# Causal attention in a decoder kernel: rotary projection with even and odd features in two halves of one bank

## The reference, cut to what matters

```python
def _rope(x, freqs):
    xr, xi = x[..., ::2], x[..., 1::2]          # even and odd features of a head
    yr = xr * cos(freqs) - xi * sin(freqs)
    yi = xr * sin(freqs) + xi * cos(freqs)
    return stack([yr, yi], axis=-1).reshape(x.shape)

KQV = einsum('bsd,ed->bse', X, W_KQV)           # X: (16, 256, 256), 16 heads of 16 features
K, Q, V = split(KQV)                            # then to (batch, head, position, feature)
Q, K = _rope(Q, freqs), _rope(K, freqs)
scores = einsum('bhqd,bhkd->bhqk', Q, K) / sqrt(16), -inf above the diagonal
heads = einsum('bhqk,bhkd->bhqd', softmax(scores), V)
return einsum('bsd,ed->bse', heads_joined, W_O)
```

## Time and profile before

| what | value |
|---|---|
| time before | 4390.62 us, median of 3 executions (4387.88 to 4397.72) |
| profiled execution, its own time | 4384.22 us |
| its span | 4382.0 us |
| granted TensorE clock, mean of the span | 0.896 |
| busy over the span | PE 3550.0 us (81%), DVE 3046.5 us (70%), ACT 1118.1 us (26%), POOL 1578.6 us (36%) |
| causal stage | from the first weight load at 33.0 us to the last write of x_all at about 576 us |

### The profile page before, as it was taken

One profiled execution on the slowest core, in us unless ns is written; L12 is line 12 of the kernel. 1 busy time (PEld: TensorE's weight loads), 2 busy tenths in 40 slices (PEclk: granted clock), 3 DMA queues, 4 the chain that ended last, 5 costly groups with the idle time before them and its releaser, 6 DMA issues. The chain is left out here.

```text
span 4382.0 us, 100620 instructions
## 1 busy us (share of the span) xinstructions
PE 3550.0 (81%) x34160; PEld 2968.7 (68%) x34161; DVE 3046.5 (70%) x11891; ACT 1118.1 (26%) x2415; POOL 1578.6 (36%) x1612
## 2 busy tenths in 40 slices
PE   3999938885688998898999896788868866799991
PEld 2777725554688888888888885455546654699991
DVE  5777735665999999999999995799973444422222
ACT  0333314442222222222222220444431110122220
POOL 1222212220666666666666674323200000111115
PEclk9999968887799999999999998899987965899995
DMA  4333333332000000000000000433310014455555
GB/s 118 93 90 94 81 73 96 90 95 85 2 2 3 2 2 2 2 2 2 2 2 2 3 2 20 108 91 93 91 29 20 7 33 125 134 181 182 180 180 158
DMA packets 246561, 282.58 MB, mean 64 GB/s; under 512 B 35225, under 2 KB 188321, under 8 KB 245825
## 3 DMA queue, kind: packets, MB, share of 16 engines
q1 hardware_dynamic: 239681, 260.04, 20.7%
q0 software_dynamic: 6528, 17.83, 1.4%
HBM read 201.31 MB, written 76.48 MB: 63 GB/s over the span
## 5 line engine op out<-in xcount | busy, mean ns | idle before, releaser
L1100 POOL TENSOR_TENSOR peer_hot_v<-peer_hot_e,peer_parts 80x512 bf16<-80x512 bf16 x768 | 1038.0, 1378 | 494.5 <-DVE peer_hot_e L1138 467.1
L946 PE MATMUL peer_ps_u<-peer_up,peer_g 128*128 128x256 f32 x2048 | 531.6, 406 | 0.6 <-DVE x_all L1255 0.6
L927 PEld LDWEIGHTS peer_ps_h<-peer_xnT,peer_down 128*128 128x128 f32 x4096 | 511.6, 197 | 17.5 <-DMA peer_down<-in_peer_down 2.8
L927 PE MATMUL peer_ps_h<-peer_xnT,peer_down 128*128 128x128 f32 x4096 | 511.0, 279 | 2.4 <-DMA peer_down<-in_peer_down 2.4
L937 PE MATMUL peer_ps_w<-peer_hot_v,peer_hot_u 80*128 80x32 bf16 x12288 | 348.0, 177 | 191.3 <-DVE peer_g L1150 96.1
L937 PEld LDWEIGHTS peer_ps_w<-peer_hot_v,peer_hot_u 80*128 80x128 bf16 x12288 | 335.2, 97 | 219.4 <-DVE peer_hot_u L1142 119.8
L946 PEld LDWEIGHTS peer_ps_u<-peer_up,peer_g 128*128 128x128 f32 x2048 | 396.9, 203 | 51.6 <-issue 1.0
L2050 POOL DMA_INDIRECT x_all<-moe_xn_rows,moe_column x72 | 68.3, 949 | 1007.8 <-DVE moe_column L2118 1002.8
L1023 ACT ACTIVATE peer_g<-peer_ps_h 128x512 f32<-128x512 f32 x256 | 152.9, 597 | 892.5 <-PE peer_ps_h L927 892.5
L1142 DVE TENSOR_TENSOR peer_hot_u<-peer_count,peer_uvT 80x2048 bf16<-80x2048 bf16 x256 | 344.8, 1347 | 0.0
L1959 PE MATMUL moe_ps_h<-x_all,moe_w 128*128 128x128 f32 x2304 | 270.1, 276 | 0.0
(11 more groups left out here) (364 smaller groups left out, 7215.5 us busy)
## 6 DMA issues: line engine op xcount, KB each, us to landing
moe_w<-in_moe_w SPq DMA_DIRECT2D x144, 512.0 KB, 4.4
causal_qs<-causal_qscratch SPq DMA_DIRECT2D x32, 384.0 KB, 3.8
cross_qs<-cross_qscratch SPq DMA_DIRECT2D x32, 384.0 KB, 3.5
band_qs<-band_qscratch SPq DMA_DIRECT2D x32, 384.0 KB, 3.8
moe_y_rows<-x_all SPq DMA_DIRECT2D x72, 128.0 KB, 1.7
moe_w<-in_moe_w SPq DMA_DIRECT2D x8, 1024.0 KB, 6.8
causal_qscratch<-causal_part SPq DMA_DIRECT2D x32, 192.0 KB, 2.0
causal_kscratch<-causal_part SPq DMA_DIRECT2D x32, 192.0 KB, 2.0
```

The source lines that it names most:

```text
L927: mm = nc.tensor.matmul(ps_h[:, n % 2, k * P:(k + 1) * P], down[:, c, 4 * n + k, :], xnT[:, par, c, :], start=(c == 0), stop=(c == DC - 1))
L946: mm = nc.tensor.matmul(ps_u[:], g[:, par, v, :], up[:, v, :], start=(v == 0), stop=(v == EV - 1))
L1100: ins = nc.gpsimd.tensor_tensor(hot_v[0:SEL, n % RING, part], hot_e[0:SEL, n % RING], w, ALU.mult)
```

## The change

Weights of q and k are laid out so that the first 128 columns are the even features of all 16 heads and the last 128 the odd ones. One job now covers all of q, and one all of k: its products with even and with odd features fill the two halves of one bank (four f32 products a job, as before, but two jobs a batch element where there were four). The projections with swapped weights and their two weight loads go. VectorE multiplies the whole bank (128x512) by a cosine and by a sine table, then forms the even half by a subtraction and the odd half by an addition, each 128x256, f32 only. The bf16 high part is no longer a second addition on VectorE: ScalarE copies it, 128x512, from `full`, and GpSimd waits for ScalarE's semaphore `high_ready`. GpSimd's three operations are 128x512 in place of 128x256. The jobs stand at steps 2 and 5 instead of 2, 4, 6 and 8. The scratch writes keep their number and size. Each `stack` issues eight DMAs of half the size where it issued four, and the two stacks of element 1 have an additional wait on `s1_done`. The order of the 96 rows of `qs` and `ks` changes alike on both sides.

```diff
-    JOBS = [(qk, c) for c in range(DC) for qk in range(2)]
+    JOBS = [(0, None), (1, None)] if rope else [(qk, c) for c in range(DC) for qk in range(2)]
+    WIDE = DC * S if rope else S
...
-    STACKED = 16 * (1 + len(KRUNS))
+    STACKED = 16 * (1 + len(KRUNS)) * (DC if rope else 1)
...
-        names = ["wq", "wqs", "wk", "wks", "wv"] if rope else ["wq", "wk", "wv"]
-        w = {n: sb(n, [P, DC, D]) for n in names}
+        w = {n: sb(n, [P, DC, D]) for n in ("wq", "wk", "wv")}
...
-        PROJECT, OUT, VALUES, STACK = (2, 4, 6, 8), 10, 12, 10
+        PROJECT, OUT, VALUES, STACK = (2, 5) if rope else (2, 4, 6, 8), 10, 12, 10
...
+                    if rope:
+                        for e in range(DC):
+                            half = slice(e * S, (e + 1) * S)
+                            if qk == 0:
+                                for slot, slots, a in QRUNS:
+                                    sp.dma_start(qscratch[par, e, slot:slot + slots].rearrange("s p t -> p s t"),
+                                                 part[:, j, a:a + 1, half].broadcast_to((P, slots, S))).then_inc(parts_out, 16)
+                            else:
+                                sp.dma_start(kscratch[par, e].rearrange("s p t -> p s t"),
+                                             part[:, j, :, half]).then_inc(parts_out, 16)
+                        return
...
+                    if rope:
+                        if isinstance(b, int) and b == 1:
+                            sp.wait_ge(s1_done, CH * c + 1)
+                        def rows(ap):
+                            return ap.rearrange("s (r h) t -> (s r) h t", h=HEADS)[:, mine, :]
+                        for e in range(DC):
+                            at = e * ROWS // DC
+                            sp.dma_start(qs[at:at + ROWS // DC, par, mine, :], rows(qscratch[par, e])).then_inc(stacked[c], 16)
+                            for slot, slots, a in KRUNS:
+                                sp.dma_start(ks[at + slot * HALFD:at + (slot + slots) * HALFD, par, mine, :],
+                                             rows(kscratch[par, e, a:a + slots])).then_inc(stacked[c], 16)
+                        return
...
-                    mine = [("wq", "wqs"), ("wk", "wks")] if rope else [("wq",), ("wk",)]
-                    for k, name in enumerate(mine[qk]):
+                    for k, part_of in enumerate(range(DC) if rope else (chunk,)):
                         for c in range(DC):
                             mm = nc.tensor.matmul(ps_p[:, (j + 1) % 2, k * S:k * S + n],
-                                                  w[name][:, c, chunk * P:(chunk + 1) * P], src[:, par, c, :],
+                                                  w[("wq", "wk")[qk]][:, c, part_of * P:(part_of + 1) * P], src[:, par, c, :],
...
                     if rope:
+                        act.wait_ge(proj_used, NJ * b + j + 1)
+                        wait(act, split_ready, NJ * b + j - 1)
+                        wait(act, parts_out, OUTS * b)
+                        nc.scalar.activation(part[:, j, 0, :], full[:, j % 2, :], ACT.Copy).then_inc(high_ready, 1)
                         return
...
-                    pool.wait_ge(proj_used, NJ * b + j + 1)
+                    pool.wait_ge(high_ready if rope else proj_used, NJ * b + j + 1)
...
-                    nc.vector.tensor_tensor(rot[:, j % 2, 0, :], bank[:, 0:S], tab[cs][:], ALU.mult)
-                    steps.link(nc.vector.tensor_tensor(rot[:, j % 2, 1, :], bank[:, S:2 * S], tab[sn][:], ALU.mult))
+                    by_cos, by_sin = rot[:, j % 2, 0], rot[:, j % 2, 1]
+                    nc.vector.tensor_tensor(by_cos, bank, tab[cs][:].unsqueeze(1).broadcast_to((P, DC, S)), ALU.mult)
+                    steps.link(nc.vector.tensor_tensor(by_sin, bank, tab[sn][:].unsqueeze(1).broadcast_to((P, DC, S)), ALU.mult))
 
                     wait(dve, split_ready, NJ * b + j - 1)
-                    wait(dve, parts_out, OUTS * b)
-                    for dst in (full[:, j % 2, :], part[:, j, 0, :]):
-                        ins = nc.vector.tensor_tensor(dst, rot[:, j % 2, 0, :], rot[:, j % 2, 1, :], ALU.add)
-                    ins.then_inc(proj_used, 1)
+                    nc.vector.tensor_tensor(full[:, j % 2, 0:S], by_cos[:, 0, :], by_sin[:, 1, :], ALU.subtract)
+                    nc.vector.tensor_tensor(full[:, j % 2, S:2 * S], by_sin[:, 0, :], by_cos[:, 1, :],
+                                            ALU.add).then_inc(proj_used, 1)
...
+def _even_odd(np, wt):
+    v = wt.reshape(wt.shape[0], HEADS, HD // 2, 2)
+    return np.transpose(v, (0, 3, 2, 1)).reshape(wt.shape)
```

More of the change, by code:

```diff
@@ L155, in attention_stage @@
     CH = HEADS // DC
-    JOBS = [(qk, c) for c in range(DC) for qk in range(2)]
+    JOBS = [(0, None), (1, None)] if rope else [(qk, c) for c in range(DC) for qk in range(2)]
     NJ = len(JOBS)
+    WIDE = DC * S if rope else S
+    HALFD = HD // 2
     QRUNS = [(0, 3, 0), (3, 2, 1), (5, 1, 2)]
@@ L188, in attention_stage @@
             maskf = sb("maskf", [P, 2, P])
-            rot = sb("rot", [P, 2, 2, S])
+            rot = sb("rot", [P, 2, 2, DC, S])
             nload += 5
@@ L207, in attention_stage @@
         xnT = sb("xnT", [P, 2, DC, S])
-        full = sb("full", [P, 2, S])
-        rest = sb("rest", [P, S])
-        part = sb("part", [P, NJ, 3, S], BF16)
+        full = sb("full", [P, 2, WIDE])
+        rest = sb("rest", [P, WIDE])
+        part = sb("part", [P, NJ, 3, WIDE], BF16)
         qs = sb("qs", [P, 2, HEADS, S], BF16)
@@ L239, in attention_stage @@
         proj_used = sem("proj_used")
+        high_ready = sem("high_ready")
         rest_ready = sem("rest_ready")
@@ L625, in project @@
                     qk, c = JOBS[j]
-                    n = S if qk == 0 else KS
+                    n = WIDE if qk == 0 or rope else KS
                     src, high = full[:, j % 2, 0:n], part[:, j, 0, 0:n]
-                    pool.wait_ge(proj_used, NJ * b + j + 1)
+                    pool.wait_ge(high_ready if rope else proj_used, NJ * b + j + 1)
                     wait(pool, split_ready, NJ * b + j)
@@ L669, in project @@
                     qk, c = JOBS[j]
-                    bank = ps_p[:, (j + 1) % 2, :]
+                    bank = ps_p[:, (j + 1) % 2, :].rearrange("p (e t) -> p e t", e=DC)
                     cs, sn = ("cosk", "sink") if qk else ("cosq", "sinq")
                     wait(dve, proj_used, NJ * b + j - 1)
-                    nc.vector.tensor_tensor(rot[:, j % 2, 0, :], bank[:, 0:S], tab[cs][:], ALU.mult)
-                    steps.link(nc.vector.tensor_tensor(rot[:, j % 2, 1, :], bank[:, S:2 * S], tab[sn][:], ALU.mult))
+                    by_cos, by_sin = rot[:, j % 2, 0], rot[:, j % 2, 1]
+                    nc.vector.tensor_tensor(by_cos, bank, tab[cs][:].unsqueeze(1).broadcast_to((P, DC, S)), ALU.mult)
+                    steps.link(nc.vector.tensor_tensor(by_sin, bank, tab[sn][:].unsqueeze(1).broadcast_to((P, DC, S)), ALU.mult))
                     wait(dve, split_ready, NJ * b + j - 1)
-                    wait(dve, parts_out, OUTS * b)
-                    for dst in (full[:, j % 2, :], part[:, j, 0, :]):
-                        ins = nc.vector.tensor_tensor(dst, rot[:, j % 2, 0, :], rot[:, j % 2, 1, :], ALU.add)
-                    ins.then_inc(proj_used, 1)
+                    nc.vector.tensor_tensor(full[:, j % 2, 0:S], by_cos[:, 0, :], by_sin[:, 1, :], ALU.subtract)
+                    nc.vector.tensor_tensor(full[:, j % 2, S:2 * S], by_sin[:, 0, :], by_cos[:, 1, :],
+                                            ALU.add).then_inc(proj_used, 1)
                 def values(self, b, par):
@@ L2224, in _chunk_bias @@
     return _rows_first(np, b).reshape(DC, P).T
-def _pairs_swapped(wt):
-    return wt.reshape(wt.shape[0], -1, 2)[:, :, ::-1].reshape(wt.shape)
+def _even_odd(np, wt):
+    v = wt.reshape(wt.shape[0], HEADS, HD // 2, 2)
+    return np.transpose(v, (0, 3, 2, 1)).reshape(wt.shape)
 def _constants(np):
@@ L2238, in _constants @@
     cos, sin = np.cos(angle).astype(f), np.sin(angle).astype(f)
-    ct, st = np.zeros((HD, S), f), np.zeros((HD, S), f)
-    ct[0:HD:2], ct[1:HD:2] = cos, cos
-    st[0:HD:2], st[1:HD:2] = -sin, sin
-    ct, st = np.repeat(ct, HEADS // DC, 0), np.repeat(st, HEADS // DC, 0)
+    ct, st = np.repeat(cos, HEADS, 0), np.repeat(sin, HEADS, 0)
     c |= {"cosk": ct, "sink": st, "cosq": ct * f(0.25), "sinq": st * f(0.25)}
@@ L2261, in _lay_out @@
     wk, wq, wv = (m.T for m in np.split(v["L0_attn_W_KQV"], 3, axis=0))
-    a |= {"causal_wq": _rows_first(np, wq), "causal_wk": _rows_first(np, wk), "causal_wv": wv,
-          "causal_wqs": _rows_first(np, _pairs_swapped(wq)), "causal_wks": _rows_first(np, _pairs_swapped(wk)),
+    a |= {"causal_wq": _even_odd(np, wq), "causal_wk": _even_odd(np, wk), "causal_wv": wv,
           "causal_wo": _slot_rows(np, v["L0_attn_W_O"].T)}
```

## The result

The kernel after the change takes 4398.62 us (median, 4391.02 to 4405.58), the kernel before on the same chip 4390.89: a ratio of 1.0019, 95% interval 1.0012 to 1.0027. That is 8 us slower, within the range of the forecast, on the other side of no change than its 4387.1. The profiled execution has a span 20.2 us longer than that of the earlier trace rows.

A forecast was written before the change was run, and what follows sets the result against it. TensorE was taken to set the causal stage's pace. Gains of 11 + 1.4 + 1.5 = 14 us, less 10.5 for clock falls, left 3.5 us: 4387.1 us for the median, range 4366 to 4401.

The forecast's parts named there:

- the stop at find 7: Behind the second job, TensorE stands still 1.75 us until VectorE, after the rotation, takes the maximum of head 5.
- the 1.5 us of each fall: After an emptier stretch behind the second job, TensorE's clock drops to a mean of 0.55 for 3.4 us, losing 1.5 us.
- `head` 5: Behind the first job, TensorE waits 0.35 us for an exponential queued behind ScalarE's copy.
- `weigh`: Behind the first job, TensorE waits 0.3 us for `normalise` on VectorE to free `ps_o`.
- `head` 8: Behind the second job, TensorE waits another 0.35 us for the exponential of head 6, behind ScalarE's copy.
- the sum: Without any clock change: 11 us from 14 elements, 1.4 from loads and 1.5 at the start, 14 us less.
- the clock term: Falls of TensorE's clock behind the second job: 0 to 21 us over 14 elements, taken as 7 falls, 10.5 us.
- The start: At the causal stage's start, a shorter rotation of element 1 frees VectorE's chain: 1.5 us of gain, between 0 and 3.
- The loads: Ahead of the stage, two weight loads of 256 KB go: 1.4 us less, on the path.
- The clock falls in every element: Rival, causal stage: 14 falls of 1.5 us make it 7 us slower, 4398, or 4425 if longer; chance 0.13.
- The clock holds: Rival, causal stage: no falls come and the whole 14 us stay, 4376.6; chance 0.26.
- The stacks come late: Rival: finds wait for stacks; above 1.9 us of delay each further microsecond costs 14; chance 0.03.

The follow-up runs named there:

- e1: Kernel after the change, with idle products on TensorE ahead of find 7 (20) and head 8 (5) in macros with projections; ratio to before 0.9980.
- e3: Kernel before the change, with the products of the swapped weights left out and VectorE's work kept; ratio to before 0.9910.
- e2: Kernel after the change, with the second job at step 4 in place of 5; ratio to before 0.9945.
- e11: Second launch of the kernel after with its second job at step 4 in place of 5, otherwise unchanged; ratio to before 0.9955.
- e4: Kernel after the change, with the bf16 high part made by GpSimd and not by ScalarE; ratio to before 0.9998.
- e5: Kernel after the change, run again unchanged; ratio to before 1.0021.
- e6: Kernel after the change, with eight idle products ahead of each element's first job, making it 0.43 us later; ratio to before 1.0037.
- e7: Kernel after the change, with VectorE's two multiplications of a job cut to 128x256, leaving out half of the rotated products; ratio to before 0.9962.
- e8: Kernel after with jobs at steps 2 and 4, and the subtraction, addition and ScalarE's copy one step later; ratio to before 1.0016.
- e9: As e8, with GpSimd's split of the first job begun only behind VectorE's addition of the second; ratio to before 1.0042.
- e10: As e2, with GpSimd's split of the first job begun only behind VectorE's addition of the second; ratio to before 1.0006.
- e12: Kernel after the change, with the second job at step 8 in place of 5; ratio to before 1.0041.

## Why the prediction was wrong

**What held.** The two jobs, the 2.0 us of VectorE (2.17 forecast), the stop at find 7 (1.73 us from start to start for the 1.75 forecast, 1.56 of them as waiting), the 29.9 us from `out` to `out` (29.7 to 29.9) and the 1.5 us of each fall: as written. Measured the same way, `head` 5 costs 0.37 us (0.35 forecast), `weigh` 0.32 (0.3) and `head` 8 only 0.21 (0.35), in all 2.6 of the 2.8. The stacks take 3.0 us of SyncE for 3.5 and hold nothing up in the steady state. Up to the `out` that closes the last projections the kernel is 0.8 us ahead (511.99 to 512.81) in spite of 8 falls of 1.5 us, the last of them with 0.4 us still to come, so 12.4 without them, where the sum had 14.

**The failed step: the clock term counted the falls among the projections' elements alone.** "This can happen in none of the 14 elements or in all: 0 to 21 us" left out the elements behind them, so the term was 10.5 us where 16.6 came (e1, without the falls, gives back 15.9), and the 4.6 us behind those elements alone are more than the 3.5 of gain that were forecast. That 8 falls came for the 7 put in is luck: 7 was the middle between none and all, not read from a row. From that `out` to the end of the stage the kernel after loses 5.0 us over code that did not change: 0.4 are the rest of the fall at 509.4, and 4.6 come of two more, at 550.4 and 570.9 us, where before had none. The second lies on the last `out`, whose sixteen products take 6.02 us for the 3.72 of before. The waits ahead of them are the same (1.48 and 1.88 us ahead of line 575, line 550 before), at times 0.4 and 1.3 us apart. Timelines of PE at the last `out`, before and then after:

```profile
571.11 3.72 PE L561 MATMUL causal_ps_p<-causal_wo,causal_onT 128*128 128x256 f32 x16 [0.78 <-DVE causal_onT L738]
```

```profile
573.00 6.02 PE L586 MATMUL causal_ps_p<-causal_wo,causal_onT 128*128 128x256 f32 x16 [0.78 <-DVE causal_onT L768]
```

The windows of 1.61 us busy in both kernels, above, show equal work at two clocks. Over the runs the tail, from that `out` to the end of the stage, takes 64.1 us in before, e1 and e3, 65.6 in e2 and e11, and 68.1 to 69.7 in after, e4, e5, e6, e7 and e8. So it can lose 4 us where no element with projections falls (e7) and nothing where before's own products were halved (e3). None of these runs edits the tail; it only begins at another time in each. What in that decides over a fall stays open, as no run shifted the tail alone.

**Smaller misses of the same sum.** One fall more than 7 costs 1.5 us. The start was to give 2.9 us and two elements 1.6 more; at the first `out` 0.65 is there, or 2.15 without the fall at 140.8. The loads gave 1.76, and 2.3 were there at the transposes. The first macro then gained nothing up to its stack (2.35 us sooner): its first job has a wait of 1.56 us too, at 104.03, where the sum had 0.1 with `normalise` as cover, but the first macro has no element behind it to normalise. And from the stack's first issue to the find that waits for it are 6.55 us where before had 5.41, so 1.1 us are lost with the eight issues, which the sum had at nothing; that the added issues did it is read from these rows alone. The later elements gained 0.86 us each for 0.8 and made up some 0.7. Together 1.6 us of gain missing, 1.5 of falls and 4.6 of tail make the 7.7 us between -3.5 forecast and +4.2 measured in the stage. The median is 8 us slower and not 4.2, and the other 4 us stay open: the kernel before was profiled once, and over the thirteen other profiles the ratio lies between 2 us less and 8 us more than the stage tells, less than the unchanged stages move from one profile to the next.

**The rivals.** "The clock falls in every element" gave 4398, the time that came, but with 8 falls of 14 and a tail in place of the other six: the right number by luck. "The clock holds" is e1: its stage is 11.7 us shorter than that of before, and the whole 8.8 us, 14 forecast. "The stacks come late" did not happen in the steady state, but its margin was 0.8 us and not 1.9: e9, e10 and e12 show that some three microseconds more on the way to scratch set it off, at 26 to 42 us.

As to whether the clock falls at all: filling the waits (e1) ended the falls, so the rows that spoke for falls were right, though six of the fourteen elements had the same waits and no fall. The Trainium skill, "TensorE: Matmul & The Clock Gate", section "Why this matters for your kernels", lets short gaps pass. The trace does not agree: in eight elements of after, waits of 1.56 us and less were followed by falls.

## What to carry to other kernels

When work is taken off the bounding engine, count what each piece covered: here 3.6 us went and 2.7 came back, since a longer job on VectorE stood ahead of the next maximum. Then look at what stands behind the job: one step sooner, ahead of `weigh`, the kernel is 24 and 20 us under the kernel before in two launches, where the change itself had lost 8, while three steps later missed the stacks. And a wait on TensorE can cost twice, as the wait and as the clock behind it; idle products in the wait tell the two apart. The last elements, whose own work is the same, can fall too.

## What the runs showed of the hardware

- Equal work is followed by either clock. Equal stretches of 1.61 us busy in 3.40 were followed by 0.50 in one kernel and 1.00 in the other; with the job 0.4 us later (e6) the falls went from six to four in eleven intervals; e4's waits of 1.56 us had none behind them in eleven; e2's of 1.07 us were followed by none from the first `out` on, and e10's of at most 0.7, at other times and beside waits for stacks, by 10.
- A VectorE operation with both inputs in SBUF ended only behind the GpSimd operation that it began beside: all 55 such cases of the causal stage in after, e2 and e8 ended about 0.3 us behind it. VectorE's 128x256 subtraction, 0.42 us alone, took 0.82 in e2 (281.80, GpSimd busy to 282.35), and the additions 1.37 in e8; each ended 0.27 to 0.29 us behind the end of GpSimd's operation, which itself took 1.15 to 1.21 us, against 1.15 to 1.16 alone. In the kernel after it shows at the start alone, on DVE and POOL:

```profile
64.36 1.21 DVE L709 TENSOR_TENSOR causal_full<-causal_rot 128x256 f32<-128x256 f32 x1
65.49 1.37 DVE L710 TENSOR_TENSOR causal_full<-causal_rot 128x256 f32<-128x256 f32 x1
```

```profile
64.14 1.15 POOL L662 TENSOR_TENSOR causal_part<-causal_full,causal_part 128x512 bf16<-128x512 f32 x1
65.36 1.21 POOL L664 TENSOR_TENSOR causal_part<-causal_rest,causal_part 128x512 bf16<-128x512 f32 x1
```

  The multiplications, which read PSUM and SBUF, kept their 0.69 and 0.68 us beside GpSimd (280.48 and 281.09 in e2). The Trainium skill, "SBUF — State Buffer", section "Who interferes with whom", says that a VectorE instruction with two inputs in SBUF contends with a GpSimd instruction that reads SBUF, since its second input comes through ports that the two share and lock, and that one with at most one such input does not (outside VectorE's two-port modes). The traces agree on both: 0.82 to 1.37 us for 0.42, and 0.68 us unchanged.
